# A state-space and int8-FFN block on eight cores: weight scaling moved from ScalarE to VectorE, and a small butterfly moved from GpSimd to VectorE

## What is computed

```python
x  = L0_attn_u                        # (8, 4096, 2048) f32
xn = layernorm(x)
# recurrent part
state = xn @ W_b_rank @ W_b_state     # rank 64, then 256 states
state = apply_butterfly(state, A)     # 8 levels of 2x2 factors over 256 = 2^8
s = state @ W_c_rank @ W_c_model + D_vec * xn
# int8 feed-forward: one weight scale for each output row, one activation scale for each token
w_scale = clip(max(abs(weight), axis=1), 1e-8) / 127
w_q = clip(round(weight / w_scale), -128, 127)
x_scale = maximum(max(abs(xn), axis=2) / 127, 1e-12)
x_q = clip(round(xn / x_scale), -128, 127)
g = silu(einsum(x_q, w_q) * x_scale * w_scale + bias)
out = x + s * g
```

## Time and profile before

| | us |
|---|---|
| median of 2 runs | 963.35 (959.75 to 966.94) |
| profiled execution, its own time | 952.68 |
| its span on the slowest core (core 1) | 951.1 |
| spans of the eight cores | 912.8 to 951.1 |
| VectorE busy on core 1 | 635.9 (67%) |
| TensorE busy on core 1 | 557.6 (59%) |
| ScalarE busy on core 1 | 305.7 (32%) |
| GpSimd busy on core 1 | 109.8 (12%) |

### The profile page before, as it was taken

The page is one execution under the profiler, slowest core; times in us unless marked ns, Lnnn a source line. Parts: engine busy times, 40 slices in busy tenths (PEclk is TensorE's granted clock), DMA queues, the critical chain, the costliest instruction groups (busy, mean ns, idle before and its releaser), DMA issues.

```text
span 951.1 us, 7805 instructions; the slowest of 8 cores (912.8 to 951.1 us)
## 1 busy us (share of the span) xinstructions
PE 557.6 (59%) x2368; PEld 239.5 (25%) x2368; DVE 635.9 (67%) x706; ACT 305.7 (32%) x255; POOL 109.8 (12%) x200
## 2 busy tenths in 40 slices
PE   0011011100010398994898698988689889999990
PEld 0001000000000143341333243433234333444440
DVE  1434134573534479995898899989689987767662
ACT  0122123552524233433353343533243442111100
POOL 3820000001011001000011100110001110000000
PEclk9999999999996598997999998989879999999996
DMA  8359999987684557689869868858996885863531
GB/s 162 98 173 171 103 161 204 262 187 146 123 149 90 120 123 218 185 121 234 217 179 252 222 192 215 239 176 198 171 247 188 232 229 202 184 230 118 215 137 46
DMA packets 134956, 169.24 MB, mean 178 GB/s; under 512 B 110210, under 2 KB 110274, under 8 KB 124674
## 3 DMA queue, kind: packets, MB, share of 16 engines
q0 software_dynamic: 16272, 75.78, 27.9%
q10 hardware_dynamic: 14194, 67.77, 25.4%
q1 hardware_dynamic: 104448, 25.19, 21.4%
HBM read 101.86 MB, written 58.72 MB: 169 GB/s over the span
## 4 chain that ended last, share of the span: by engine, by line
DMA 27%; DVE 26%; PE 19%; issue 10%; ACT 10%; POOL 4%; ACTq 2%; DVEq 1%; POOLq 0%
DMA vh<-v 18%; PE ffnps L584 17%; DMA wdh<-y 5%; DMA o<-Wff 4%; DVE y L451 4%; DVE stats L355 4%; DVE y L490 3%; DVE s L474 3%; ACT v L233 3%; DVE stats L353 3%; ACT v L245 2%; ACT y L195 2%; ACT v L237 2%; DVE s L469 2%; DVE stats L410 1%
## 5 line engine op out<-in xcount | busy, mean ns | idle before, releaser
L584 PE MATMUL ffnps<-wT,slabB 128*128 128x512 f16 x1024 | 236.4, 393 | 39.1 <-DVE y L490 39.1
L584 PE MATMUL ffnps<-wT,slabA 128*128 128x512 f16 x1024 | 239.0, 396 | 33.8 <-DVE y L490 33.8
L584 PEld LDWEIGHTS ffnps<-wT,slabB 128*128 128x128 f16 x1024 | 101.6, 101 | 173.3 <-issue 64.0
L584 PEld LDWEIGHTS ffnps<-wT,slabA 128*128 128x128 f16 x1024 | 102.1, 101 | 170.3 <-issue 62.7
L259 ACT ACTIVATE y<-y 128x2048 f16<-128x2048 f16 x32 | 61.2, 1912 | 254.8 <-DVE y L490 241.3
L233 ACT ACTIVATE v<-u 128x2048 f16<-128x2048 f16 x32 | 61.2, 1911 | 207.5 <-DMA vh<-v 206.7
L490 DVE SCALAR_TENSOR_TENSOR y<-ffnps,stats,brep 128x1024 f16<-128x1024 f32 x64 | 79.9, 1276 | 37.5 <-PE ffnps L584 37.5
L353 DVE TENSOR_REDUCE stats<-u 128x1 f32<-128x2048 f16 x32 | 73.0, 2280 | 33.3 <-DMA u<-u 33.1
L474 DVE TENSOR_TENSOR s<-z3ps,s 128x2048 f16<-128x2048 f32 x32 | 73.3, 2292 | 16.2 <-PE z3ps L567 13.0
L451 DVE SCALAR_TENSOR_TENSOR y<-s,stats,y 128x2048 f16<-128x2048 f16 x32 | 75.2, 2351 | 5.4 <-ACT y L259 2.2
L555 PE MATMUL z3ps<-slabA,wbr 128*64 128x512 f16 x64 | 16.1, 409 | 104.0 <-DMA slabA<-vh 104.0
(11 more groups left out here) (72 smaller groups left out, 297.0 us busy)
## 6 DMA issues: line engine op xcount, KB each, us to landing
o<-u ACTq DMA_DIRECT2D x32, 1024.0 KB, 6.3
out<-o POOLq DMA_DIRECT2D x32, 1024.0 KB, 4.9
u<-u POOLq DMA_DIRECT2D x32, 512.0 KB, 9.3
o<-Wff ACTq DMA_DIRECT2D x16, 1024.0 KB, 9.0
vh<-v POOLq DMA_DIRECT2D x32, 512.0 KB, 10.0
vr<-vh ACTq DMA_DIRECT2D x32, 512.0 KB, 8.3
wdh<-y POOLq DMA_DIRECT2D x16, 512.0 KB, 9.1
wT<-wdh SPq DMA_TRANSPOSE x64, 6.3
```

What stands on the lines that cost most here:

```text
L584: PE.sig(reg, tensor.matmul(ffnps[:, og * 512:(og + 1) * 512], slab[(c // 4) % 2][:, dch, (c % 4) * 128:(c % 4 + 1) * 128], wT[:, dch, og ...
```

## The change

ScalarE's pass over each weight chunk (L195) is left out. VectorE does it, as a tensor_scalar from `o32` (f32) into `y16` (f16) between `WINV` and the rounding, under the name `dv:vws:oc`; it waits for `wh:oc-2` there. ScalarE's queue reloads `o32` when `dv:vws:oc` is done. The butterfly leaves GpSimd's block and stands in VectorE's block between weight chunks 1 and 2, with two instructions for each half of a level where there were three. TensorE's transpose of the result waits for it there.

```diff
             def quant(oc):
-                w(f"dv:wsinv:{oc}")
-                w(f"ld:w:{oc}")
-                if oc >= 2:
-                    w(f"wh:{oc - 2}")
-                SC.sig(reg, scalar.activation(
-                    out=y16[:, oc % 2, :], in_=o32[:, oc % 2, :],
-                    func=ACT.Identity, scale=stats[:, oc % 4, WINV:WINV + 1]),
-                    f"sc:vw:{oc}")
                 if oc + 2 < DCH:
-                    scalar.wait_ge(SC.sem, SC.n)
-                    w(f"dv:wmax:{oc}")
+                    w(f"dv:vws:{oc}")
                     W[oc % 2].sig(reg, scalar.dma_start(
...
-                DV.sig(reg, vector.reciprocal(out=so(WINV), in_=so(WS)),
-                       f"dv:wsinv:{oc}")
-                w(f"sc:vw:{oc}")
+                DV.sig(reg, vector.reciprocal(out=so(WINV), in_=so(WS)))
+                selfw()
+                if oc >= 2:
+                    w(f"wh:{oc - 2}")
+                DV.sig(reg, vector.tensor_scalar(out=y16[:, oc % 2, :],
+                                                 in0=o32[:, oc % 2, :],
+                                                 scalar1=so(WINV), scalar2=None,
+                                                 op0=ALU.mult), f"dv:vws:{oc}")
+                selfw()
                 w("dv:mw")
...
+                if oc == 1:
+                    w("sc:arepe")
+                    w("ld:stage")
+                    cur, nxt = wbsA, wbsB
+                    for lvl in range(8):
+                        s = 2 ** (7 - lvl)
...
+                        for j in range(2):
...
+                            DV.sig(reg, vector.tensor_scalar(
+                                out=o, in0=x1, scalar1=a1, scalar2=None,
+                                op0=ALU.mult))
+                            selfw()
+                            DV.sig(reg, vector.scalar_tensor_tensor(
+                                out=o, in0=x0, scalar=a0, in1=o,
+                                op0=ALU.mult, op1=ALU.add))
+                        selfw()
+                        cur, nxt = nxt, cur
+                    DV.sig(reg, vector.engine_nop(), "dv:bfly")
...
-            w("gp:bfly")
+            w("dv:bfly")
```

More of the change, by code:

```diff
@@ L210, in urload @@
                 else:
-                    w(f"sc:vw:{14 + cc}")
-                    w(f"dv:wmax:{14 + cc}")
+                    w(f"dv:vws:{14 + cc}")
                 UR[cc % 2].sig(reg, scalar.dma_start(
@@ L434, in _ @@
                 selfw()
+                if oc == 1:
[4 more added lines that the diff above has]
+                        s = 2 ** (7 - lvl)
+                        vsrc = cur.ap().rearrange("p (nb two s) -> p nb two s",
+                                                  two=2, s=s)
+                        vdst = nxt.ap().rearrange("p (nb two s) -> p nb two s",
+                                                  two=2, s=s)
+                        x0, x1 = vsrc[:, :, 0, :], vsrc[:, :, 1, :]
+                        for j in range(2):
+                            a0 = arep[:, (4 * lvl + j):(4 * lvl + j + 1)]
+                            a1 = arep[:, (4 * lvl + 2 + j):(4 * lvl + 3 + j)]
+                            o = vdst[:, :, j, :]
+                            DV.sig(reg, vector.tensor_scalar(
[8 more added lines that the diff above has]
+                    DV.sig(reg, vector.engine_nop(), "dv:bfly")
             for cc in range(min(LAG, C)):
@@ L635, in _ @@
             uload(1)
[L636 to L664, removed]
             for oc in range(DCH):
```

## The result

The first series gave 945.42 us with the change (median of 11 runs, 924.64 to 1003.42) against 953.31 before (10 runs). The ratio is 0.9769, 95% interval 0.9715 to 0.9822: 22 us, where 13 were forecast. Two more series of the same kernel, on two chips and each with executions of the kernel before beside it, gave 947.02 against 950.19 (ratio 0.9987, 0.9912 to 1.0062) and 939.92 against 947.92 (0.9885, 0.9807 to 0.9962). The ratios leave slow executions out, which cuts the long tail of this kernel and makes them depend on where the cut falls. So the 22 us were not repeated. I therefore also took a steadier figure, the mean span over all eight cores and all executions: 917.6 us with the change (30 executions, standard error 1.3) against 924.2 before (45 executions of the later series, 0.9). That is 6.6 us, with a standard error of 1.6.

The account below looks back on a forecast made before the run. The slowest core's weight phase, ahead of the fronts, was taken as the bound. Gains of 6.4 (chunk 3), 5.7 (free steps) and 1.0 (waiting steps) sum to 13.1, taken as 13 us off 963.35: 950 us, range 936 to 966.

Parts of the forecast that it names:

- The costs of the moved work: VectorE in the weight phase: 1.28 us for each chunk's new pass and 12.0 us for the butterfly.
- the three rates: VectorE's new f32 pass over 2048 columns: 0.75, 1.28 or 2.35 us by the rate assumed; 1.28 was taken.
- The reduce of chunk 3: VectorE in the weight phase: this reduce was to come at 53.0 us for 59.37, 6.4 us earlier.
- The free step: A weight chunk step without DMA waits: 6.21 us for 7.03, 0.82 less; seven such steps give 5.7 us.
- The six waiting steps: Chunk steps after chunk 3 that wait for DMA: gain 0 if throughput limits, up to 2.8 us if latency; 1.0 taken.
- all 13 steps: Core 1's chunk steps from the reduce of chunk 3 to L353: 129.8 us, 38.4 of it DMA waits.
- The step that failed: Between weight phase and first feed-forward matmul on core 1: 137.2 us, unchanged, so gains pass to the end nearly whole.
- Its own signs: Wrong if the slowest core's weight-phase DMA waits change by over 10 us or the main loop moves from 625 us.
- Rival 1: Weight phase: every chunk step after chunk 3 gains 0.82 us, 17.1 us in all, 946 us; chance 0.20 beyond the forecast.
- Rival 2: A slow f32 pass, or DMA limits in weight phase and main loop, leave nothing gained: 962 us; chance 0.12.
- Rival 3: Weight stores and loads collide with the transposes: one more 19.1 us wait gives 969 us, two 988; chance 0.09.
- Rival 4: GpSimd's weight stores held up by VectorE's new pass, up to 1.28 us, three times: 4 us, so 954; chance 0.04.

Follow-up runs that it names:

- pass_only: The change with the butterfly left on GpSimd, only the scaling pass moved to VectorE: 951.28 us against 952.47 before.
- bfly_only: The kernel before with only the butterfly moved to VectorE, the pass left on ScalarE: 957.03 us against 952.47 before.
- bfly_twice: The changed kernel with the eight butterfly levels done twice on VectorE: 950.77 us against 947.02 for the change.
- pool_mix: The change with the butterfly back on GpSimd, one level at a time between stores, and ScalarE's evictions later: 923.11 us against 952.47 before.
- late_tr: The change with the weight transposes started only after the stores of chunks 14 and 15 have landed: 921.92 us against 952.47 before.
- both: pool_mix joined with the two added waits of late_tr: 918.84 us against 950.19 before.

## Why the prediction went as it did

- **The costs of the moved work held.** The pass was put at 1.28 us and took 1.286; the butterfly at 12.0 and took 11.9. The middle of the three rates that the prediction weighed for the pass was a choice that came out. The reduce of chunk 3 was to gain 6.4 us and gained 6.5. The free step came to 6.29 for 6.21: the new pass starts some 0.1 us later behind its waits than I had from the earlier trace rows.
- **The six waiting steps** were booked at 1.0 us of gain together, since a shorter ring was thought to wait longer there. They gained like the others: the waits stayed at 19 to 20 us in the mean, so all 13 steps are 10.9 us shorter for the 6.7 booked. This term was too small.
- **The step that failed** is "from there core 1 takes 137.2 us to its first feed-forward matmul", with its conclusion that what ends the weight phase sooner comes out nearly one for one. On core 1 the stretch grew to 146.5 us, in the mean from 134.7 to 141.5. The nine fronts themselves got longer (120.5 to 127.5), 5.1 us of it in waits for token loads. The transposes are issued to their end at 224 to 226 us, whether the weight phase ends at 171 or at 154, so they stand beside the fronts for 70 us in place of 55. That this is the cause of the longer waits is argued. For it: over the 64 profiled cores of before, the change, `pass_only`, `bfly_only`, `bfly_twice` and `pool_mix` these waits grow with that stretch (correlation 0.72). Against: in `late_tr`, with 112 us side by side, the fronts took 125.0 us, no longer than with the change. What passes is the shift of chunk 3 (`bfly_twice`: 12 in, 12 out). The two errors, 4.2 us too little and 6.8 too much, nearly cancel at the first matmul: 10.6 for 13. That the total came so close there is luck.
- **The size in the span**, 6.6 us in the mean and 9 in the median time, is half to two thirds of the 13. In the profiled executions themselves 11.6 us arrive (mean spans 925.0 and 913.4). The main loop behind the first matmul differs by a few us between single profiles (618.8 before, 615.4 to 621.2 after), so whether the last 4 us are lost there or are scatter stays open.
- **Its own signs.** The main loop of core 1 stayed near 625 us (620.9). The waits of the weight phase on the slowest core shrank by 15.8 us, which the prediction had named as a sign that it is wrong. By the means (20 and 19 us) that is a different draw and not the change.
- **The 22 us of the first series** belong to no step. The distance of slowest core and mean core is 25 us in the executions of before and 22 to 30 in the three series of the change. I had worked on core 1 of one profile, with 38 us of waits where the mean was 20; the metric takes the maximum of eight such draws.
- **Rival 1** (all steps gain) was right in the weight phase (17.4 us at the first L353 for its 17.1) and wrong at the end. **Rival 2**, in which the DMA waits of the main loop take the gain, was right that DMA waits take a part, but they were those of the fronts. **Rival 3** did not come in the profiles: the waits kept their mean. One execution of the change reached 1003 us, with one core at 1001.9 and the others at 903 to 937; it has no profile, and the highest before was 977, so a rare collision can't be ruled out. **Rival 4**: the lock of VectorE and GpSimd was there, on the butterfly in `pass_only`; the stores' issue took 0.53 us before and after.

## What to carry to other kernels

When a stream of transfers runs beside a phase, what the phase gains can be lost behind it, and starting the stream later or ordering it anew can be worth more than the phase itself: look at when the stream ends, before and after, not only at the waits of the engines. Here two added waits on SyncE's queue gained 12.8 us in the mean span, on top of the 6.6 of the whole change. When the metric is the slowest of eight cores whose waits differ from one execution to the next, sum over the mean core, and measure in the mean too.

## What the hardware did that I had not expected

The 64 DMA transposes of the weights took 171 us on core 1 before and 177 with the change, and 110 on core 0 of `late_tr`, where they began behind the weight phase's loads and stores; in the means over the cores it is 153, 159 and 106. On the slowest core of each profile a load of a weight chunk landed in a median of 9.0 us before and in 5.6 in `both`, a store in 9.1 and 4.1.
